# Where group ranges, weights and x's first turns stand in a four-layer graph network, and dense blocks put into two waits of TensorE

## The reference

```python
# layer 0: degrees, scaled neighbours
h = x @ W0;  deg = segment_sum(1, dst) + 1;  dinv = rsqrt(deg)
x = layernorm(x + relu(segment_sum(h[src] * dinv[src] * dinv[dst], dst) + own + b0))
# layer 1: weighted neighbours
x = layernorm(x + segment_sum(x[src] * w, dst) @ W_rel.T + b_rel + x @ W_root.T)
# layer 2: attention, 4 heads of 64
z = x @ W;  e = leaky_relu(es[src] + ed[dst]);  alpha = softmax of e over each dst
x = layernorm(x + segment_sum(alpha * z[src], dst))
# layer 3: weighted neighbours
x = layernorm(x + relu(segment_sum((x @ W3)[src] * w, dst) + b3))
```

## Time and profile before

| | us |
|---|---|
| median of three runs | 1779.27 |
| lowest and highest | 1779.17, 1781.78 |
| profiled execution | 1778.9 |
| its span, first to last instruction | 1777.1 |
| TensorE busy, matmuls | 1588.4 (89%) |
| VectorE busy | 1186.3 (67%) |
| ScalarE busy | 511.2 (29%) |
| GpSimd busy | 514.9 (29%) |
| mean granted TensorE clock | 0.962 |

### The profile page before, as it was taken

One profiled execution on the slowest core, in us unless ns is written; L12 is line 12 of the kernel. 1 busy time (PEld: TensorE's weight loads), 2 busy tenths in 40 slices (PEclk: granted clock), 3 DMA queues, 4 the chain that ended last, 5 costly groups with the idle time before them and its releaser, 6 DMA issues.

```text
span 1777.1 us, 37754 instructions
## 1 busy us (share of the span) xinstructions
PE 1588.4 (89%) x13731; PEld 1296.0 (73%) x13731; DVE 1186.3 (67%) x2739; ACT 511.2 (29%) x996; POOL 514.9 (29%) x540
## 2 busy tenths in 40 slices
PE   5779999999998999999778888888888777999998
PEld 4568787878885888888646666666666556888887
DVE  9788999999998122222279999999999876121111
ACT  0432232323231000000245555555555454000000
POOL 0032121211113000000077777777777600000000
PEclk9989999999999999999869999998998979999999
DMA  8912212121215244443144444444444421444440
GB/s 215 57 41 82 112 79 115 79 115 79 115 79 227 78 141 143 159 159 130 49 111 112 113 112 114 111 114 111 113 112 113 97 112 38 160 165 170 172 169 14
DMA packets 81220, 203.71 MB, mean 115 GB/s; under 512 B 42635, under 2 KB 57327, under 8 KB 71439
## 3 DMA queue, kind: packets, MB, share of 16 engines
q1 hardware_dynamic: 60047, 141.94, 25.5%
q0 software_dynamic: 20992, 59.37, 12.7%
HBM read 153.00 MB, written 53.57 MB: 116 GB/s over the span
## 4 chain that ended last, share of the span: by engine, by line
PE 57%; POOL 15%; DVE 13%; issue 12%; ACT 1%; DMA 1%; DVEq 1%; POOLq 0%; SPq 0%; ACTq 0%
PE bank L1232 30%; POOL ring L469 15%; PE bank L1176 9%; PE bank L1168 5%; PE bank L1161 2%; PE bank L1194 2%; DVE work L801 2%; PE bank L1318 1%; PE bank L1240 1%; DVE big L814 1%; DMA ring<-attention_rows,work 1%; PE bank L1134 1%; ACT work L590 1%; PE bank L1185 1%; DVE stats L819 1%
## 5 line engine op out<-in xcount | busy, mean ns | idle before, releaser
L469 POOL DMA_INDIRECT ring<-attention_rows,work x420 | 398.7, 949 | 150.0 <-issue 147.3
L1232 PE MATMUL bank<-big,ring 128*128 128x256 f32 x1250 | 273.0, 379 | 0.9 <-DVE x_sb L839 0.9
L1232 PE MATMUL bank<-big 128*128 128x256 f32 x1250 | 272.9, 379 | 0.0
L1232 PEld LDWEIGHTS bank<-big,ring 128*128 128x128 f32 x1250 | 236.5, 190 | 33.4 <-DVE x_sb L839 1.7
L1232 PEld LDWEIGHTS bank<-big 128*128 128x128 f32 x1250 | 236.6, 190 | 31.7
L1318 PE MATMUL bank<-work,ring 128*65 128x48 f32 x3360 | 236.7, 231 | 9.7 <-ACT work L590 8.6
L1318 PEld LDWEIGHTS bank<-work,ring 128*65 128x65 f32 x3360 | 225.8, 146 | 18.2 <-ACT work L590 16.2
L1176 PE MATMUL bank<-big 128*128 128x256 bf16 x1875 | 209.0, 273 | 0.9
L1176 PEld LDWEIGHTS bank<-big 128*128 128x128 bf16 x1875 | 181.4, 98 | 25.3 <-ACT big L512 4.6
L590 ACT ACTIVATE work<-work 128x960 f32<-128x960 f32 x84 | 161.5, 1923 | 84.3 <-DVE work L988 84.3
L1057 DVE TENSOR_TENSOR u<-bank,bias 128x256 f32<-128x256 f32 x25 | 10.6, 425 | 211.4 <-PE bank L1232 211.4
(11 more groups left out here) (214 smaller groups left out, 1979.2 us busy)
## 6 DMA issues: line engine op xcount, KB each, us to landing
adjacency<-big SPq DMA_DIRECT2D x25, 1600.0 KB, 5.2
ring<-adjacency SPq DMA_DIRECT2D x25, 1600.0 KB, 6.9
big<-adjacency SPq DMA_DIRECT2D x25, 1600.0 KB, 7.3
ring<-attention_rows,work POOLq DMA_INDIRECT x420
edge_rows<-edge_list SPq DMA_DIRECT2D x1, 4983.0 KB
x_sb<-in_x SPq DMA_DIRECT2D x1, 3072.0 KB
out_x<-xnT SPq DMA_DIRECT2D x24, 128.0 KB, 4.4
work<-attention_rows SPq DMA_DIRECT2D x168, 1.1 KB
```

The costliest lines, as they stand in the source:

```text
L469: G.indirect_dma_start(out=rows[0:EP, s, c, 0:ZG], out_offset=None, in_=ztab[:, :], in_offset=bass.IndirectOffsetOnAxis(ap=idx[:, g, c:c + ...
L1232: ins = mm(bank[:, 0:D], slots[s][:, b, :], ybuf[:, b, :], start=(b == 0), stop=(b == NT - 1))
```

## The change

It has five parts.

- **x's first turns.** Tiles 0 and 1 of x are turned, copied and multiplied inside the last batches of the count. In the loop VectorE copies tile t in turn t, from t = 2 on, and TensorE turns tile t and then multiplies tile t-1, as before.
- **The weights.** `w_rr` is copied in turns 6 and 9 of VectorE's loop, and the four pieces of the attention weights are made in turns 12, 15, 18 and 21, each behind the tile's first subtraction.
- **The group ranges** move to layer 1: VectorE's part behind layer 0's last tile and in turns 2 and 6, TensorE's in turns 1 and 4, with banks 0 and 1.
- **Layer 0's end.** SP loads slots 0 and 1 ahead of the store of the last tile. TensorE does the first ten blocks of layer 1's tile 0 between the last `relate` steps (`first_dense`, bank 5) and the other 15 behind the last one. Layer 1's banks change their turns. GpSimd clears `big1` once layer 1's second tile is done.
- **Layer 3's blocks.** A table, `blocks3`, lists for each step of the stage ahead which blocks of layer 3's tiles 0 to 2 TensorE does there, at most two per step, from step 5 (tile 0), 8 (tile 1) and 12 (tile 2), never a block younger than five steps. It comes to 23 blocks of tile 0 and 20 of tile 1. Layer 3 uses three banks (4, 5, 2).

```diff
@@ pool @@
-            pool.wait_ge(c_dense, nswb * NT)
+            pool.wait_ge(e1["dense"], 2)
             G.memset(big1[:, 0:2 * NPAD], 0.0)
@@ setup @@
+        banks3 = [banks[4], banks[5], banks[2]]
+        for step in range(NT + 3):
+            for j, begin in enumerate((5, 8, 12)):
+                while step >= begin and taken3[j] <= step - 5 and len(blocks3[step]) < PAIR:
+                    blocks3[step].append((j, taken3[j]))
+                    taken3[j] += 1
@@ sync @@
+            for t in range(NT - 1):
+                store_a(t)
+            sp.wait_ge(s_wz, 1)
+            sp.wait_ge(s_wTc, 2)
+            sp.wait_ge(b_h, NT)
+            sp.wait_ge(a_stored[0], 16)
+            load_a(slots1[0], 0, a1_loaded[0])
+            sp.wait_ge(a_stored[1], 16 * (NT // 2))
+            load_a(slots1[1], 1, a1_loaded[1])
+            store_a(NT - 1)
@@ vector @@
-            for b in range(DB // 2 + 6, DB):
+            for b in range(DB // 2 + 6, DB - 2):
                 digit_one_hots(b)
+            xT_copy(0)
+            digit_one_hots(DB - 2)
+            xT_copy(1)
+            digit_one_hots(DB - 1)
...
-            xT_copy(0)
             for t in range(NT + 2):
-                if t + 1 < NT:
-                    xT_copy(t + 1)
+                if 2 <= t < NT:
+                    xT_copy(t)
                 if t >= 2:
                     v = ys[:, (t - 2) % DEPTH, :]
                     dve.wait_ge(b_p2, t - 1)
...
+                if t in (6, 9):
+                    relation_weights(t // 9)
+                elif t in (12, 15, 18, 21):
+                    attention_weights((t - 12) // 6, (t - 12) // 3 % 2)
@@ tensor @@
+            def first_dense(blocks):
+                for b in blocks:
+                    pe.wait_ge(e0["y"], b + 1)
+                    ins = mm(out_banks[1][:, 0:D], slots1[0][:, b, :], ybuf[:, b, :], start=(b == 0), stop=(b == NT - 1),
+                             skip_group_check=True)
+                return ins
...
+                if t == NT + 1:
+                    first_dense(range(4, 7))
                 if 2 <= t <= NT + 1:
                     turn_x_next(e0, t - 2, e0["xn"])
+                if t == NT:
+                    pe.wait_ge(a1_loaded[0], 16)
+                    pe.wait_ge(e0["u"], NT - 1)
+                    first_dense(range(0, 4))
+                elif t == NT + 1:
+                    first_dense(range(7, 10))
+            first_dense(range(10, NT)).then_inc(e1["dense"], 1)
...
+                for j, b in blocks3[t]:
+                    if b == 0:
+                        pe.wait_ge(a3_loaded[j], 16)
+                    pe.wait_ge(e2["y3"], b + 1)
+                    mm(banks3[j][:, 0:D], slots3[j][:, b, :], ybuf[:, b, :], start=(b == 0), stop=False, skip_group_check=True)
```

## The result

| | before | changed kernel |
|---|---|---|
| median, us | 1779.22 | 1802.51 |
| lowest and highest of four runs | 1778.94, 1781.78 | 1801.18, 1803.24 |
| span of the profiled execution | 1777.1 | 1801.2 |
| mean granted clock of the span | 0.962 | 0.933 |
| ratio, with its 95% interval | | 1.0127 [1.0109, 1.0144] |

The change costs 23.3 us. The direction is the forecast one and the time lies in the range, but it is rival 2's time (1803) and not the forecast's (1786). It is in the range only because the range was drawn to 1804, to take in half of that rival; the size of the loss was not foreseen.

What follows compares the result with a forecast made beforehand. The scaled rows' loop was taken as held by a chain between engines, layers 1 and 3 by TensorE. Terms: +26.8 + 5 - 8.5 + 0.6 - 17.5 = +6.4 us, so 1786 us; range 1779 to 1804.

Steps and rivals of the forecast that it cites:

- rival 2: Scaled rows' loop: clock at 1.2 GHz through most of it, +22 us instead of +5, 1803 us; chance 0.15.
- Start of the loop: Scaled rows' loop: VectorE copies x's tile 2 at 57.0 us instead of 66.88, 9.9 us earlier.
- Term 1: Scaled rows' loop: one chain left, 2.92 us per tile instead of 1.46, weights exposed for 5.2 us; +26.8 us.
- Term 2: Scaled rows' loop: clock falls to 1.2 GHz for 5 to 6 tiles, +0.95 us each; +5 us (0 to 22).
- Rival 1: Scaled rows' loop: the clock holds, no gap over 1.5 us; sum +1.4, 1781 us; chance 0.24.
- Term 3: Layer 0's end: memsets no longer hold VectorE's normalising, ten dense blocks fill TensorE's waits; -8.5 us (-6 to -10).
- Term 4: Layer 1: group ranges cost VectorE nothing, but their turns and product lengthen TensorE's full queue; +0.6 us (0.3 to 2).
- Term 5: Layer 3: 43 blocks done in the stage ahead, which pays little for them; -17.5 us (-13 to -18.5).
- Rival 3: Stage ahead of layer 3: blocks lengthen VectorE's steps, 9 us of the gain lost, 1795 us; chance 0.08.
- Rival 4: Scaled rows' loop: copy not held behind the subtraction, two chains stay, edge rows end last; 1748 us; chance 0.03.

Runs made afterwards that it cites:

- the filled run: The changed kernel with four extra matmuls of 512 columns, which nobody reads, behind each turn of x in the scaled rows' loop: 1781.51 us.
- the kernel with one chain alone: The kernel before with the copy order alone: x's tiles 0 and 1 copied ahead of the scaled rows' loop, tile t in turn t: 1832.89 us.
- the kernel with the later clear: The kernel before with only GpSimd's memsets of the accumulator moved behind layer 1's second tile: 1948.97 us, ratio 0.9957, on the chip where the kernel before takes 1957.93.

## Why the prediction was right or wrong

- **Start of the loop: right.** Copy of tile 2 at 57.09, said 57.0; the first of the two products in the count took 1.92 us and not 1.13, which did not show in the start.
- **Term 1, one chain (+26.8): right.** Period 2.92 us at 2.4 GHz in the filled run, the last copy at 128.0 there (said 126.4), with one fall of the clock on the way. The weights: 90.2 us between the copies of tiles 2 and 24 are 22 x 3.87 = 85.1 and 5.1 more, said 5.2.
- **Term 2, the clock (+5, 0 to 22): the step that failed.** Measured +21.8 (48.6 - 26.8); against the filled run, which holds the clock but for one fall, the loop is 20.3 longer. The time per tile at 1.2 GHz was right (0.95 us), the number of tiles was not: all of them, where I had put 5 to 6. I took the share from a stage in which TensorE works 37.6 of 52 us and doubled it for longer gaps. But that was a share of time in a state that comes back, and here the state does not come back. The rival's own "for" named the reason, that TensorE has the least work here of any long stage; I gave it 0.15 because the only row showed recovery. The row was from another regime. With bounds of 0 and 22 and no row between, the two ends deserved the weight and the middle little. The price per tile was read from a row (63.43) whose window reads 1.00; the length is right, as the changed kernel's rows at 0.50 have 2.07 and 2.08.
- What TensorE did ahead of a fall, at 2.4 GHz: without extra matmuls it waits 1.37 and 1.58 us per tile, and the clock falls behind that (69.74 and 72.66 in the kernel with one chain alone). With one extra matmul it waits 1.26 us and the clock holds over many tiles (first line below); its two falls in the loop stand at the pieces of the attention weights, where the wait is 2.37 and 2.17 us (second line), but two other pieces with waits of 2.53 and 2.37 us cost no fall. The changed kernel's fall, at 58, comes behind a wait of 2.23 us. Rival 1's "for", that no gap is over 1.5 us, had left out the waits behind the weights.

```profile
85.14 1.13 PE L1139 MATMUL bank<-ring,xnT 128*128 128x256 f32 x4 [1.26 <-DVE xnT L737]
```

```profile
92.11 1.81 PE L1139 MATMUL bank<-ring,xnT 128*128 128x256 f32 x4 [2.37 <-DVE xnT L737]
```

  The Trainium skill (TensorE: Matmul & The Clock Gate, "HAM oscillation — how this bites in real kernels") ties the fall to long idle gaps between matmuls. The runs agree only in part: most of the falls stand at the longer waits, but the kernel with one chain alone lost the clock behind waits of 1.37 and 1.58 us and did not get it back in 82 us. By that section it would have been rival 1's 1781, which came only with the waits filled. Why the low level stays in the unfilled loop and is left again in the filled one is not shown beyond this.
- **Term 3, layer 0's end (-8.5): right,** -9.9; 6.6 of it the clear, 3.3 the blocks (I had 6 less 2 to 3 pushed back, and the blocks' 4.3 saved).
- **Term 4, layer 1 (+0.6): right,** +0.5.
- **Term 5, layer 3's blocks (-17.5): right,** -17.7. Rival 3 did not happen: VectorE kept its 2.37 us per tile, and the full TensorE held its clock.
- **Attention, not in the sum:** +2.2 (549.4 us for 547.2 from first gather to last sums). It isn't touched by the change; the other kernels on such chips have 546.9 to 549.6, so I take it as the spread of the stage; no run settles it.
- Rival 4 (1748, two chains) did not happen in the changed kernel, but it is what the change would have been with the copy's place kept: 1744.7. The working for it (copy of tile 24 at 94.3, then the edge rows at 96.7) held in size: 92.7 and 97.0. In that trace the edge rows were ready at 94.1 and VectorE's last subtractions ended the wait; in the second trace of the same kernel it was the edge rows (99.0, turn at 99.1).

## What to carry to other kernels

In a loop whose tile passes through several in-order engines, count how many tiles are in flight by reading where the next tile's first step stands relative to the wait for this tile's last. Moving one copy behind one wait halved it here and cost more than all the other edits together gave. If TensorE then waits in every tile and no row shows such a loop, as here, price its work at 1.2 GHz for the whole stretch and at 2.4 GHz as the other case, not as a mean; and if TensorE is a link of the chain, work that nobody reads in its waits is a cheap test, and sometimes a remedy.

## What the runs showed of the hardware

The clock has a persistent low state in a regular loop: 3.87 us per tile with TensorE at work 2.5 of it, 0.50 granted for some 90 us. With one more matmul of 0.39 us per tile it fell twice in the loop and came back after 6.8 and 3.4 us; with four it fell once, for 3.4 us.

Chips differ in it. On one chip the unchanged kernel takes 1957.93 us (1955.73 to 1959.83, eight runs), on the others 1779 to 1780. Up to layer 0 the traces are alike (last copy of the loop at 99.4 for 99.6), the adjacency loop is some 14 us longer, layers 1 and 3 are alike, and the attention takes 710.6 us instead of 547. A window of the attention, first of the kernel with the later clear on that chip, then of the kernel with two chains on another:

```profile
1000.00:1100.00 100.00, 84.11 (x686) 62.11 (x686) 69.93 (x180) 41.88 (x49) 56.72 (x60) 0.75 0.33 86
```

```profile
1000.00:1100.00 100.00, 85.25 (x907) 63.34 (x905) 92.55 (x241) 52.65 (x64) 75.60 (x81) 0.95 0.43 112
```

A quarter less work is done in the same time, and TensorE looks equally busy: again the low clock hides in the busy share. Whether the low clock is the cause or the result of slower groups there, no run tells. One thing more differs in the traces: on that chip GpSimd's gathers of the attention wait 135.3 to 148.6 us in all, in 60 to 66 waits of up to 2.4 us, for an event that the profile calls only "remote"; on the others it has no such wait. For this study the difference between chips only meant that times of different chips could not be set beside each other.
